# A state-space block on one Trainium2 core: step sizes from one fp32r product with a contraction of 98 rows

## What is computed

```python
xn = layernorm(x)
u, gate = split(xn @ W_in.T)            # D = 1024 each
u = silu(conv4(u) + conv_b)
dt, B, C = split(u @ Wx.T, [32, 48])    # R = 32, N = 16, N = 16
dt, B, C = rmsnorm(dt), rmsnorm(B), rmsnorm(C)
delta = softplus(dt @ Wdt.T + dt_bias)  # "z" is the argument of softplus
state = exp(delta * A) * state + (delta * u) * B     # over time, 1024 x 16 states
y = sum_n(state * C) + u * D_param
s = (y * silu(gate)) @ W_out.T
out = x + s * silu(ffn(xn))             # ffn: hidden 1376
```

## Time and profile before

| | |
|---|---|
| median of 3 runs | 1154.21 us (1153.61 to 1157.15) |
| profiled execution | 1153.85 us, its span 1151.9 us |
| PE busy, matmuls | 92%, 5072 |
| DVE busy | 91%, 1260 instructions |
| POOL busy | 84%, 549 |
| ACT busy | 60%, 1114 |
| granted PE clock over the span | 0.973 of 2.4 GHz |
| DMA | 160.66 MB, 40% of 16 engines |

### The profile page before, as it was taken

The page is one execution under the profiler, slowest core; times in us unless marked ns, Lnnn a source line. Parts: engine busy times, 40 slices in busy tenths (PEclk is TensorE's granted clock), DMA queues, the critical chain, the costliest instruction groups (busy, mean ns, idle before and its releaser), DMA issues.

```text
span 1151.9 us, 14914 instructions
## 1 busy us (share of the span) xinstructions
PE 1060.7 (92%) x5072; PEld 755.3 (66%) x5072; DVE 1051.8 (91%) x1260; ACT 691.1 (60%) x1114; POOL 970.7 (84%) x549
## 2 busy tenths in 40 slices
PE   6989988889999999999999999998999999999767
PEld 5767765666667776666757776576857787555444
DVE  4599999999999999899999999899999999888895
ACT  5657546866665756677565846476565665465440
POOL 3567997999987898889978899889988899879961
PEclk9979999899999999999999999999999999999878
DMA  4646663533324644342224543443223443334310
GB/s 140 229 133 222 203 224 114 177 120 134 103 100 148 211 143 161 127 155 98 104 93 156 187 157 142 146 146 129 99 95 128 152 164 113 123 117 167 124 59 36
DMA packets 46550, 160.66 MB, mean 139 GB/s; under 512 B 5355, under 2 KB 5611, under 8 KB 37004
## 3 DMA queue, kind: packets, MB, share of 16 engines
q1 hardware_dynamic: 46332, 159.66, 40.3%
q10 hardware_dynamic: 144, 0.07, 0.0%
HBM read 135.33 MB, written 24.38 MB: 139 GB/s over the span
## 4 chain that ended last, share of the span: by engine, by line
PE 47%; DVE 22%; POOL 15%; issue 11%; ACT 5%; DMA 0%; DVEq 0%; SPq 0%; POOLq 0%; ACTq 0%
PE pj L1186 14%; DVE sb_h L1125 12%; PE hT L1478 9%; PE pj L1387 7%; POOL sb_dBu L855 7%; DVE sb_yT L1040 5%; PE pj L1421 5%; PE pj L1452 3%; POOL sb_yT L815 3%; PE pj L1204 2%; PE pj L1496 2%; PE pj L1191 2%; DVE sb_un L932 2%; POOL sb_un L786 1%; ACT dA L626 1%
## 5 line engine op out<-in xcount | busy, mean ns | idle before, releaser
L855 POOL TENSOR_TENSOR sb_dBu<-sb_v,sb_bb 128x1024 f32<-128x1024 f32 x254 | 602.6, 2385 | 51.5 <-DVE sb_h L1125 37.6
L1125 DVE TENSOR_TENSOR_SCAN sb_h<-dA,sb_dBu 128x512 f32<-128x512 f32 x512 | 597.8, 1212 | 21.6 <-ACT dA L626 11.8
L626 ACT ACTIVATE dA<-sb_delta,sb_apar 128x512 f32<-128x512 f32 x510 | 345.2, 689 | 260.9 <-DVE sb_h L1125 256.8
L1186 PE MATMUL pj<-sb_x_hi,sb_w_sp 128*128 128x512 f32 x1208 | 343.8, 408 | 19.0 <-DVE sb_un L932 12.3
L1478 PE MATMUL hT<-sb_ident,sb_h 128*128 128x128 f32 x2048 | 286.2, 281 | 53.1 <-DVE sb_yT L1040 43.1
L1478 PEld LDWEIGHTS hT<-sb_ident,sb_h 128*128 128x128 f32 x2048 | 241.6, 144 | 138.3 <-issue 47.2
L1186 PEld LDWEIGHTS pj<-sb_x_hi,sb_w_sp 128*128 128x128 f32 x1208 | 219.7, 191 | 82.8 <-issue 24.4
L1040 DVE SCALAR_TENSOR_TENSOR sb_yT<-hT,sb_cs,sb_yT 128x512 f32<-128x512 f32 x335 | 239.0, 739 | 32.4 <-PE hT L1478 31.7
L815 POOL TENSOR_TENSOR sb_yT<-sb_yT,sb_part 128x512 f32<-128x512 f32 x141 | 181.0, 1284 | 40.1 <-ACT sb_part L723 39.9
L723 ACT ACTIVATE sb_part<-hT,sb_cs_act 128x512 f32<-128x512 f32 x141 | 96.4, 684 | 127.4 <-PE hT L1478 125.1
L1186 PE MATMUL pj<-sb_x_lo,sb_w_sp 128*128 128x512 f32 x604 | 166.1, 397 | 0.0
(11 more groups left out here) (145 smaller groups left out, 782.8 us busy)
## 6 DMA issues: line engine op xcount, KB each, us to landing
sb_w_sp<-w_cache SPq DMA_DIRECT2D x55, 1024.0 KB, 4.8
sb_ring<-w_ring SPq DMA_DIRECT2D x67, 512.0 KB, 3.7
sb_bb<-b_rows SPq DMA_DIRECT2D x128, 256.0 KB, 4.1
w_cache<-sb_w_sp SPq DMA_DIRECT2D x19, 1024.0 KB, 4.9
sb_xio<-x SPq DMA_DIRECT2D x7, 1024.0 KB, 6.9
out<-sb_xio SPq DMA_DIRECT2D x3, 1024.0 KB, 5.7
sb_xio<-x SPq DMA_DIRECT2D x4, 256.0 KB, 3.5
out<-sb_xio SPq DMA_DIRECT2D x4, 256.0 KB, 2.0
```

The costliest lines, as they stand in the source:

```text
L626: nc.scalar.activation(dA[g % 2][:, :], delta[:, j, :], ACT.Exp, scale=apar[:, j, n:n + 1]).then_inc(dA_done, 1)
L855: nc.gpsimd.tensor_tensor(dBu[:, dbu_buffer(s), :, :], v[:, j:j + 2, :], bb[:, i % B_RING, :].unsqueeze(1).to_broadcast([P, 2, T]), ALU.mu ...
L1125: nc.vector.tensor_tensor_scan(h[:, i % 2, 2 * part + e, :], dA[g % 2][:, :], dBu[:, dbu_buffer(s), e, :], 0.0, ALU.mult, ALU.add).then_in ...
L1186: done = nc.tensor.matmul(bank[:, :], w[:, kk * P:(kk + 1) * P], xs[:, kk, :], start=(p == 0), stop=(p == len(products) - 1))
```

## The change

z is computed in one pass of fp32r. `dtB` has 98 rows: three copies of dt and two of ones. Rows 0 to 63 are rounded to fp32r, rows 64 to 95 get the rest (dt less its rounded value, one subtraction by DVE, `rest_dt`); `wdt` holds rounded weights in rows 0 to 31 and 64 to 95, their rest in rows 32 to 63, and the rounded bias and its rest in the last two. The rests of the weights are made once, before step 0, by ACT, POOL and DVE. `apply_rms` writes dt three times; squaring takes one instruction instead of two. B's rows are copied by ACT into the tile `xio` and stored from there; the second half is stored after row 1 instead of row 7, and the load of x waits for it. `Z0_AT` is 55, 56, 57, 58, with the banks as before. The first product of each half waits for the subtraction too.

```diff
-G = R + 1
-FN = F + 1
+G = 3 * R + 2
+FN = G + N
-Z0_AT, Z0_BANK = (54, 55, 57, 58), (3, 2, 3, 2)
+Z0_AT, Z0_BANK = (55, 56, 57, 58), (3, 2, 3, 2)
...
-    after = {("row", 7): "b_half"}
+    after = {("row", 1): "b_half"}
...
-        wdt = sb("wdt", [G, D])
+        wdt = sb("wdt", [G, D], fp32r)
...
-        dtB = sb("dtB", [G + N, T])
+        dtB = sb("dtB", [G, T], fp32r)
...
+        b_rows = xio[3 * R:FN, 0, :]
+        wdt_raw = S[0:G, 0:D // T, :].rearrange("p a t -> p (a t)")
...
-                sp.dma_start(b_dram[q], dtB[G:G + N, :]).then_inc(b_out[q], 16)
+                sp.dma_start(b_dram[q], b_rows[G - 3 * R:, :]).then_inc(b_out[q], 16)
...
                     if after == "x":
+                        sp.wait_ge(b_out[1], (b + 1) * 16)
...
-                nc.scalar.activation(nrm[:, t, 0:R], p_ssm[:, :, 0:R], ACT.Square)
-                nc.scalar.activation(nrm[:, t, G:FN], p_ssm[:, :, R:F], ACT.Square).then_inc(sq_done, 1)
+                nc.scalar.activation(nrm[:, t, 0:F], p_ssm[:, :, 0:F], ACT.Square).then_inc(sq_done, 1)
...
-                    nc.scalar.activation(nrm[:, t, 0:R], ssm[:, t, 0:R], ACT.Copy, scale=ms[:, 2, t, 0:1])
+                    nc.scalar.activation(nrm[:, t, 0:3 * R].rearrange("p (q r) -> p q r", r=R),
+                                         ssm[:, t, 0:R].unsqueeze(1).to_broadcast([P, 3, R]), ACT.Copy, scale=ms[:, 2, t, 0:1])
...
-                nc.scalar.copy(dtB[:, :], bank[0:G + N, :]).then_inc(dtT_done, 1)
+                nc.scalar.copy(dtB[:, :], bank[0:G, :]).then_inc(dtT_done, 1)
+                if not (isinstance(c, int) and c < 2):
+                    act.wait_ge(out_dma, (c - 1) * 16)
+                nc.scalar.copy(b_rows[:, :], bank[3 * R:FN, :]).then_inc(dtT_done, 1)
...
+            nc.scalar.copy(wdt[:, :], wdt_raw).then_inc(wh_done, 1)
             act.wait_ge(ssm_ps, 1)
...
+            act.wait_ge(wl_done, 2)
+            nc.scalar.copy(wdt[3 * R:3 * R + 1, :], wdt_raw[3 * R:3 * R + 1, :]).then_inc(wl_done, 1)
             gate_tanh(0, 0, pj[0])
...
+            second = slice(R, 2 * R)
+            pool.wait_ge(wh_done, 1)
+            pool.wait_ge(lo_done, len(FIRST))
+            nc.gpsimd.tensor_tensor(wdt[second, :], wdt_raw[second, :], wdt[second, :].bitcast(fp32), ALU.subtract).then_inc(wl_done, 1)
+            pool.wait_ge(wl_done, 2)
...
+            def rest_dt(c, bank):
+                dve.wait_ge(dtT_done, 2 * c + 1)
+                low = slice(2 * R, 3 * R)
+                nc.vector.tensor_tensor(dtB[low, :], bank[low, :], dtB[low, :].bitcast(fp32), ALU.subtract).then_inc(dtl_done, 1)
...
+            dve.wait_ge(wh_done, 1)
+            ends = slice(3 * R, G)
+            nc.vector.tensor_tensor(wdt[ends, :], wdt_raw[ends, :], wdt[ends, :].bitcast(fp32), ALU.subtract).then_inc(wl_done, 1)
             rms_squares(0)
...
             gate_silu(0, 0, pj[0])
+            rest_dt(0, dA[0])
...
+                    if s == S_DTT + 3:
+                        rest_dt(b + 1, pj[3])
...
-                    pe.wait_ge(dtT_done, c + 1)
+                    pe.wait_ge(dtT_done, 2 * c + 2)
+                    pe.wait_ge(dtl_done, c + 1)
...
-        "w_dt": np.concatenate([get("L0_attn_Wdt").T, get("L0_attn_dt_bias")[None]]),
+        "w_dt": np.concatenate(3 * [get("L0_attn_Wdt").T] + 2 * [get("L0_attn_dt_bias")[None]]),
```

More of the change, by code:

```diff
@@ L251, in build @@
         dtT_done = sem("dtT_done")
+        dtl_done = sem("dtl_done")
+        wh_done = sem("wh_done")
+        wl_done = sem("wl_done")
         cs_done = sem("cs_done")
@@ L293, in build @@
         last_ps = sem("last_ps")
-        consts = [(cw, conv_w), (cb, conv_b), (wx, w_x), (wdt, w_dt), (apar, a_par), (dpar, d_par)]
+        consts = [(cw, conv_w), (cb, conv_b), (wx, w_x), (wdt_raw, w_dt), (apar, a_par), (dpar, d_par)]
         N_INIT = 7
@@ L375, in _ @@
                     for dst, src in consts:
-                        sp.dma_start(dst[:], src).then_inc(const_in, 16)
+                        sp.dma_start(dst if dst is wdt_raw else dst[:], src).then_inc(const_in, 16)
                     sp.dma_start(lnw[:, :], ln_w.partition_broadcast(P)).then_inc(const_in, 16)
@@ L379, in _ @@
                     keep(N_MADE + p - W_RING - 2, p % HI_RING)
-            sp.wait_ge(dtT_done, 1)
+            sp.wait_ge(dtT_done, 2)
             write_b(0)
@@ L438, in sequence @@
                     elif what == "b_rows":
-                        sp.wait_ge(dtT_done, b + 2)
+                        sp.wait_ge(dtT_done, 2 * (b + 2))
                         write_b(0)
@@ L536, in apply_rms @@
                 for t in range(TC):
-                    nc.scalar.activation(nrm[:, t, 0:R], ssm[:, t, 0:R], ACT.Copy, scale=ms[:, 2, t, 0:1])
-                    scaled = nc.scalar.activation(nrm[:, t, G:G + N], ssm[:, t, R:R + N], ACT.Copy, scale=ms[:, 2, t, 1:2])
+                    nc.scalar.activation(nrm[:, t, 0:3 * R].rearrange("p (q r) -> p q r", r=R),
+                                         ssm[:, t, 0:R].unsqueeze(1).to_broadcast([P, 3, R]), ACT.Copy, scale=ms[:, 2, t, 0:1])
+                    scaled = nc.scalar.activation(nrm[:, t, G:FN], ssm[:, t, R:R + N], ACT.Copy, scale=ms[:, 2, t, 1:2])
                 scaled.then_inc(nrm_done, 1)
@@ L908, in _ @@
             nc.vector.memset(shares[:, :, 1:3], 1.0 / N).then_inc(init_done, 1)
-            nc.vector.memset(nrm[:, :, R:G], 1.0).then_inc(init_done, 1)
+            nc.vector.memset(nrm[:, :, 3 * R:G], 1.0).then_inc(init_done, 1)
             xT_bank = [pj[2], pj[3], pj[2], pj[3]]
@@ L1196, in transpose_dt @@
                 for t in range(TC):
-                    done = nc.tensor.matmul(bank[0:G + N, t * P:(t + 1) * P], nrm[:, t, 0:G + N], ident[:, :],
+                    done = nc.tensor.matmul(bank[0:FN, t * P:(t + 1) * P], nrm[:, t, :], ident[:, :],
                                             start=True, stop=True)
@@ L1202, in to_delta @@
                 if j == 0:
-                    pe.wait_ge(dtT_done, c + 1)
+                    pe.wait_ge(dtT_done, 2 * c + 2)
+                    pe.wait_ge(dtl_done, c + 1)
+                    if isinstance(c, int) and c == 0:
+                        pe.wait_ge(wl_done, 3)
                 nc.tensor.matmul(bank[:, :], wdt[:, j * P:(j + 1) * P], dtB[0:G, :],
@@ L1332, in misc @@
                         j = Z0_AT.index(s)
-                        if j == 1:
+                        if j == 0:
+                            pe.wait_ge(dtl_done, b + 2)
+                        elif j == 1:
                             pe.wait_ge(sg_done, (b + 1) * KD + JH)
```

2 lines of the change are left out of this document (1 added, 1 removed).

## The result

The changed kernel took 1168.37 us in the median of 4 runs (1161.63 to 1172.07) against 1153.91 us before (4 runs, 1152.4 to 1157.15): a ratio of 1.0119, 95% interval 1.007 to 1.0167. Beside other kernels later it took 1164.1 us in the median of 6 runs (1157.14 to 1171.72), ratio 1.0103 [1.0065, 1.0141]. So it is slower by 1.0 to 1.2%, where the forecast was 1160.5 us, +0.5%, in a range of 1152 to 1167: the first comparison lies above the range, the second within it. The profiled execution took 1171.19 us, its span 1169.2 us, and is one of the longer ones.

A forecast was written before the change was run, and what follows sets the result against it. No single engine bounds it (PE, DVE, POOL busy 84 to 92%); what counts is which wait ends last. -3.0 + 4.8 + 3.9 + 0.7 = +6.4 us: 1160.3 profiled, 1160.5 median, range 1152 to 1167.

The forecast's parts named there:

- the start: Before the first step, splitting W_dt on POOL and DVE and wider ACT writes: +0.7 us, from -0.3 to +1.5.
- the clock: At three boundaries, PE's idle at step 57 lowers the granted clock: nothing to +2.7 us each, taken 1.3, together +3.9.
- late z: Second-half z products, steps 5 to 8 of each sequence: -1.0 us in the first, -0.65 each in three others, together -3.0.
- The gap around the product: 0.39 us around each late z product's two passes goes with 98 rows: PE step 3.87 us, otherwise 4.26.
- Early z, DVE up to step 59: First three sequences: low part of dt adds 0.65 us, the 1.41 us wait goes; DVE arrives some 1.36 us earlier.
- The new wait: PE's z products at steps 57 and 58 wait for DVE; DVE stalls 1.6 and 0.7 us; net +4.8 over three boundaries.
- (a): Rival: the stall at the boundaries comes but the clock holds, +2.5 us, 1156.5 us; chance 0.22.
- (d): Rival: the clock stays at 1.2 GHz through both boundary stalls and step 59, +16 us, 1170 us; chance 0.10.
- (b): Rival: boundary stall hidden as DVE or PE runs ahead, -6.4 us at best, about 1149.5 us; chance 0.13 with (c).
- (c): Rival: PE's saving counts in full, 28 steps of 1.0 us and more, 1126 us; chance 0.13 together with (b).
- (e): Rival: no effect over the whole kernel, the two sides cancel, 1154 us; chance 0.07.

The follow-up runs named there:

- the run with 33 rows: The changed kernel with the late z products cut from 98 rows to 33, low parts left out, still one fp32r pass: 1163.36 us in one profile.
- the run with PE kept busy: The changed kernel with useless fp32r products ahead of the waiting z products, ten at step 57, five at step 58: 1156.29 us, ratio 1.0032 to before.
- the kernel with both moves: The changed kernel with ACT's and DVE's early z work one step earlier and POOL's W_dt splitting behind its powers: 1145.12 us, ratio 0.9927 to before.

## Why the prediction was right and wrong

The direction and the mechanism at the boundaries were right, the size was not: +6.4 us forecast, 11.9 measured by the second comparison (1.0103 times 1153.8) and 13.7 by the first (1.0119), whose median of 1168.4 us lies above the range. Two terms failed: the start, put at +0.7 and measured at +4.7, because I placed POOL's new subtraction beside the wrong instruction of DVE; and the clock, put at +3.9 and measured at +6.1. Start, late z and boundaries below add up to 4.7 - 3.2 + 10.4 = 11.9, or 12.5 with the late z of the first sequence taken against the mean of three profiles, as the start is. What the first comparison has beyond that is within what the clock draws by chance: the profiled run of it lost 5.9 us so. Term by term, with the mean of what the profiles show:

**Late z** (-3.0): -1.1 and three times -0.7, so -3.2. Right in size and in its cause; the step on PE came out at 3.84 us (taken: 3.87), and the wait for ACT at step 13 took back what I said. In the first sequence the unchanged kernel's two other profiles are 0.8 us shorter in that stretch too, so only some -0.5 of the -1.1 may be the change's own (against the mean of the three), -2.6 in all.

**The gap around the product.** Right: it went, and the run with 33 rows shows 0.41 us for it where I had 0.39. (I took two passes of 0.43 us off; the row that I named, six passes in 2.68 us, has 0.45 each and leaves 0.36.) The rule that I named (the Trainium skill, TensorEngine Tiling (Array Packing), Key Properties, a change of tiling mode drains the engine) agrees with that.

**Early z, DVE up to step 59.** Right: the wait of 1.41 us at step 58 went, and the low part of dt put the next scan 0.72 us later (317.26 to 317.98 in after), where I had 0.65.

**The new wait** (+4.8): with the clock held the boundaries cost 4.3 us, 1.4 each where I had 1.6. PE's idle was 2.90 to 3.28 us (I had 3.5), and DVE's second wait 0.50 (0.7). The 0.15 us that I gave PE to wake came from no row; it started 0.06 us after L1147 had ended (329.24, 329.30). The kernel of before with the later steps alone shows that the placing makes it.

**The clock** (+3.9): too small, the second step that failed. I took 1.3 us as the middle between nothing and 2.7; it was 2.0 each (10.4 less 4.3, over three). The middle of two outcomes was no good value here: in after all three boundaries fell. At the second the fall lasted through all six down passes (5.29 us), as at the far end of my range. Between 45 and 1125 us of the twelve profiles PE idles 42 times for 2.9 us or more after work at full clock, and all 42 have the fall, in the idle or at most 1.4 us after PE went on, as the earlier trace rows had shown; of the six waits of 1.66 us in the kernel before with later steps, three have it. I had the row and did not give it full weight.

**The start** (+0.7, from -0.3 to +1.5): the step that failed most. Before has step 5 at 0, -3.0 and -3.8 in the three profiles of that start, mean -2.3; the six profiles with POOL's L849 in its place have 3.7, 1.9, 1.0, 3.6, 1.6 and 2.6, mean 2.4; so +4.7 us. The three with L849 moved have -2.7, -2.6 and -3.7, mean -3.0, below before. I placed the two-engine contention at the wrong instruction. I had DVE's own new subtraction beside POOL's (+0.55), whereas POOL's stood beside the last tile of u, on which PE's ssm products wait: DVE's second L1026 ended 0.55 us after POOL's. That delay of 1.96 us is the price of the earlier trace rows (3.44 against 1.23, 2.2 us) at a place on the path, and it opened a gap of 1.65 us on PE in front of a stretch that had been unbroken, so the clock fell for the x product on which ACT's tanh waits, with the scaling of dt behind it in ACT's queue. Moving L849 takes all of these away together; no run shows what each is worth alone. A wait, a clock fall and a queue behind it: 0.7 became 4.7. I had called the one such place; it wasn't. In the same trace the first of the two L996 took 1.78 us beside POOL's L780, and the second 0.69 alone, so before itself showed the price at the very pair beside which L849 came to stand.

**The basis.** The one profile of before was one draw. Its start was 2.3 us behind the mean of three, and its last sequence 2.1 us ahead of it. The meeting in the earlier trace rows was part of the draw: in the kernel's two other profiles DVE's L1018 came before POOL's L855 and took 1.22 us. That the two nearly cancel was luck; a range built on one profile of this kernel is some 5 us too narrow for each such place.

**Rivals.** (a), stall without the clock, is what the run with PE kept busy shows (+4.3 for the boundaries), not what after does. (d), the clock low through both stalls, did not come: at the second boundary of after it was low through all of the first stall's six passes, but back at 1.00 ahead of the second wait (four passes in 1.88 us). It comes true at the third boundary of the fp32 kernel with the later steps. (b), the stall hidden, is what the moved work reaches: -3.2 and -2.1 us for late z and boundaries. (c) and (e) are out.

**What stays open:** why the second boundary has the longer fall in all four profiles that have the stall of after (about 6.8 us against 3.4), and why the kernel with both moves draws no fall in steps 20 to 46 of the last sequence while others with the same waits there do. The idle is the same (1.92 to 1.95 us for L1074 at that place in after, in before and with both moves); in after the clock fell behind it, in the two others it didn't. So is how often the kernel with PE kept busy loses its clock all the same.

## What to carry to other kernels

Follow a new wait on an in-order queue by what stands behind it: here the waiting product was 0.3 us of work, and the six passes and eight transposes behind it made the loss; moving them ahead, or the producer one step earlier, each removed it. Price the low clock as a second cost of the same stall, at its full size if a comparable gap in the trace shows it. And when work is added "in a quiet place", look at which instruction of the engine that it contends with (here DVE, for POOL's work) it will stand beside, and whether that one is on the path, not only at its own engine's idle time; then take a second profile of the kernel before, for one profile does not show which of its gaps cost by chance.

## What the runs showed of the hardware

- Behind short gaps of PE the granted clock falls to 0.50 (1.2 GHz) or stays, by chance. Behind 1.66 us in the fp32 kernel with the later steps it held at the first boundary and fell at the second; the same code with the same waits differs by 5.9 us in one place between two executions of the kernel before. The executions that take longer have the lower mean clock (1171.19 us: 0.956; 1161.63 us: 0.971). The Trainium skill, TensorE: Matmul & The Clock Gate, What's actually happening, calls the ramp from the low to the full clock at a kernel's start run-variable; these traces show the same in mid-kernel. It also puts the ramp's penalty at less than 1% of a typical kernel's span; here the low clock at the boundaries is 6 us of 1164, below 1% too, and yet half of all that the change cost.
- Beside POOL's subtraction a DVE instruction with both inputs in SBUF ended 0.55 us after POOL's, though POOL worked on 32 partitions only: 2.65 us where it takes 0.69 alone. It goes both ways, by who starts first: in the first profile of before POOL's L855 started at 58.50 and DVE's L1018 at 58.53, and they took 2.38 and 3.44 us; with the later z steps DVE started at 58.98 and POOL at 59.03, and they took 1.22 and 3.41. That such instructions contend stands in the Trainium skill (GPSIMD Engine Reference, Specifications); the time is the trace's.
- A product of 33 rows among products of 128 costs 0.41 us more than one of 98 rows with as many columns.
- Useless products in a gap made the kernel 0.7% faster than the same kernel without them (ratios 1.0032 and 1.0103); in the trace of it the clock held.
